# Graph layer with Performer mixer and two expert banks: basis parts, selection weights and the first weight piece in another order

## The reference, cut to what matters

```python
xn = layernorm(x)                                # x: 625 x 512
x  = x + gnn(xn) + mix(xn);  x = x + ffn(layernorm(x))

# gnn: two relational layers (relu between), 30 bases, 2 relations, 10000 edges
w = einsum('rb,bio->rio', att, basis)            # basis: 30 x 512 x 512
msg = where(edge_type == 0, sigmoid(x_j @ gate_w[0]) * x_j @ w[0],
                            sigmoid(x_j @ gate_w[1]) * x_j @ w[1])
out = segment_sum(msg, row) + x @ root + bias

# mix: Performer attention
k, q, v = split(layernorm_g1(xn) @ Wkqv + bkqv)
kp, qp = exp(k @ w.T - |k|^2/2) / 16, exp(q @ w.T - |q|^2/2) / 16
y = v + (qp @ (v.T @ kp).T / (qp @ sum(kp))) @ Wo + bo
y = y + gelu(layernorm_g2(y) @ W1 + b1) @ W2 + b2

# ffn: a shared expert and two banks of 8 experts, each node to one expert of each bank
```

## Time and profile before

| | |
|---|---|
| median of 3 runs | 550.5 us (549.6 to 551.97) |
| profiled execution | 551.3 us |
| its span (first to last instruction) | 549.5 us |
| granted TensorE clock, mean | 0.98 |
| TensorE busy | 501.2 us |
| VectorE, ScalarE, GpSimd busy | 250.6, 179.9, 175.0 us |
| moved by DMA | 104.66 MB |

### The profile page before, as it was taken

One profiled execution on the slowest core, in us unless ns is written; L12 is line 12 of the kernel. 1 busy time (PEld: TensorE's weight loads), 2 busy tenths in 40 slices (PEclk: granted clock), 3 DMA queues, 4 the chain that ended last, 5 costly groups with the idle time before them and its releaser, 6 DMA issues.

```text
span 549.5 us, 7975 instructions
## 1 busy us (share of the span) xinstructions
PE 501.2 (91%) x2842; PEld 372.5 (68%) x2842; DVE 250.6 (46%) x521; ACT 179.9 (33%) x366; POOL 175.0 (32%) x175
## 2 busy tenths in 40 slices
PE   2785899999999996989999999999988999999994
PEld 2342446777666644756677877777777888888883
DVE  4858871323534369332110123200275667766643
ACT  2795674222211118112220322401555123332210
POOL 2111000740503318460458150230253335533310
PEclk9997999999999998999999999999999799999998
DMA  5999997987999789657044004000020662222003
GB/s 123 420 397 413 424 421 260 366 305 232 370 411 403 259 325 372 236 202 271 1 108 160 0 1 107 14 2 0 1 78 1 255 276 78 78 76 78 1 1 94
DMA packets 27649, 104.66 MB, mean 190 GB/s; under 512 B 4152, under 2 KB 4197, under 8 KB 18908
## 3 DMA queue, kind: packets, MB, share of 16 engines
q1 hardware_dynamic: 27612, 104.16, 51.2%
HBM read 98.63 MB, written 5.51 MB: 190 GB/s over the span
## 4 chain that ended last, share of the span: by engine, by line
PE 82%; DVE 5%; DMA 4%; issue 3%; ACT 2%; SPq 2%; PEld 1%; DVEq 1%; PEldq 1%
PE ps L1235 19%; PE ps L1237 18%; PE ps L1236 18%; PE ps L1259 9%; PE ps L1596 9%; DMA ring<-in_L_gnn_basis_dram 3%; PE ps L1321 2%; PE ps L1441 2%; PE ps L1243 1%; PE ps L1499 1%; DMA out_dram<-final 1%; PEld ps L1321 1%; DVE oh_m L702 1%; ACT h_tmp L1023 1%; DVE oh_n L700 0%
## 5 line engine op out<-in xcount | busy, mean ns | idle before, releaser
L1259 PE MATMUL ps<-ring,sel_att 128*32 128x512 f32 x512 | 67.7, 616 | 11.2 <-DMA ring<-in_L_gnn_basis_dram 7.5
L602 POOL TENSOR_TENSOR ex_lo<-ex_raw,ex_hi 128x1024 fp32r<-128x1024 f32 x17 | 40.6, 2394 | 98.4 <-ACT ex_hi L1182 98.4
L852 DVE SCALAR_TENSOR_TENSOR u_lo<-ps,gates,u_hi 125x512 fp32r<-125x512 f32 x20 | 15.0, 751 | 94.1 <-ACT u_hi L1159 94.1
L1235 PE MATMUL ps<-piece_hi,ht_hi 128*125 128x512 f32 x140 | 56.1, 401 | 0.8 <-PE ps L1237 0.6
L1237 PE MATMUL ps<-piece_hi,ht_lo 128*125 128x512 f32 x140 | 55.2, 394 | 0.0
L1236 PE MATMUL ps<-piece_lo,ht_hi 128*125 128x512 f32 x140 | 55.1, 394 | 0.0
L913 DVE CAST hg_hi<-gated 128x314 fp32r<-128x314 f32 x32 | 35.6, 1113 | 32.0 <-PE ps L1237 31.4
L556 POOL CAST piece_hi<-piece_raw 128x512 fp32r<-128x512 f32 x28 | 20.4, 728 | 83.3 <-issue 60.2
L1235 PE MATMUL ps<-ht_hi,ex_hi 128*128 128x314 f32 x136 | 43.5, 320 | 0.0
L1237 PE MATMUL ps<-ht_hi,ex_lo 128*128 128x314 f32 x136 | 43.0, 316 | 0.0
L1236 PE MATMUL ps<-ht_lo,ex_hi 128*128 128x314 f32 x136 | 42.9, 315 | 0.0
(11 more groups left out here) (264 smaller groups left out, 1049.4 us busy)
## 6 DMA issues: line engine op xcount, KB each, us to landing
ring<-in_L_gnn_basis_dram SPq DMA_DIRECT2D x64, 1024.0 KB, 9.6
rel_dram<-stag SPq DMA_DIRECT2D x16, 256.0 KB, 7.9
w_raw<-rel_dram SPq DMA_DIRECT2D x8, 512.0 KB, 6.4
ex_raw<-in_L_ffn_W_sp_dram SPq DMA_DIRECT2D x16, 256.0 KB, 5.1
ex_raw<-in_L_ffn_W_fq_dram SPq DMA_DIRECT2D x16, 256.0 KB, 2.8
piece_raw<-in_L_mix_Wkqv_dram SPq DMA_DIRECT2D x3, 1024.0 KB, 8.7
route_all<-route_dram SPq DMA_DIRECT2D x1, 2512.0 KB, 12.0
piece_raw<-in_L_mix_W_dram SPq DMA_DIRECT2D x2, 1024.0 KB, 9.8
```

What stands on the lines that cost most here:

```text
L602: pool.tensor_tensor(lo, raw, hi.bitcast(F32), ALU.subtract).then_inc(ex_split, 1)
L1235: pe.matmul(target, a_hi, b_hi, start=first, stop=False, skip_group_check=skip)
L1259: last = pe.matmul(ps[32 * c:32 * c + 32, rel_bank(ch), :], sel_att[:, ch // CHUNKS, g].rearrange("p r q -> p (r q)"), ring[slot][:, c * D ...
```

## The change

Piece "k" is loaded behind part 11 rather than behind part 7, and the six bias rows behind part 32 rather than behind "k". GpSimd adds the two bias rows behind the split of "W1" rather than before that of "q". VectorE makes `sel_att` and the low half of the gate weights before it waits for the all-reduce, rather than after round 0. `k_lo` is made after VectorE's round 6 rather than its round 4. TensorE folds parts 0 and 1 before it waits for the ranges, and one part after round 0 rather than three.

```diff
@@ sync
             for i in range(4, 8):
                 load_part(i)
-            load_piece("k")
-            for n, a in enumerate((bias1, bias2, bkqv[2 * D:3 * D], bo, b2, bs2)):
-                sp.dma_start(bias_row[:, n, :], a.partition_broadcast(128)).then_inc(smalls_in, 16)
-
-            piece_after = {24: "q", 27: "v", 30: "Wo", 34: "W1", 40: "W2", 50: "root1", 62: "root2"}
+            piece_after = {11: "k", 24: "q", 27: "v", 30: "Wo", 34: "W1", 40: "W2", 50: "root1", 62: "root2"}
...
+                if i == 32:
+                    for n, a in enumerate((bias1, bias2, bkqv[2 * D:3 * D], bo, b2, bs2)):
+                        sp.dma_start(bias_row[:, n, :], a.partition_broadcast(128)).then_inc(smalls_in, 16)
@@ gpsimd
+            for name in ("q", "v", "Wo", "W1"):
+                split(name)
             pool.wait_ge(smalls_in, 16 * 6)
             own_step(pool.tensor_tensor(bias_row[:, 4, :], bias_row[:, 4, :], bias_row[:, 1, :], ALU.add))
-            for name in ("q", "v", "Wo", "W1"):
-                split(name)
@@ vector
+            dve.wait_ge(dve_own, sel_q_made)
+            dve.wait_ge(att_col_ready, 5)
+            a = sel_att[:].rearrange("p l g r q -> p (l g r) q")
+            dve.tensor_tensor(a, att_col[:]..., sel_q[:]..., ALU.mult).then_inc(sel_ready, 1)
+            dve.wait_ge(gate_w_hi, 1)
+            ...
+            dve.tensor_tensor(gate_w[:, :, 1, :], gate_ps, gate_w[:, :, 0, :].bitcast(F32), ALU.subtract).then_inc(gate_w_ready, 1)
             dve.wait_ge(bound_max, 1)
...
-                if j == 0:
-                    ...                       (the same steps)
-                if j == 4:
+                if j == 6:
                     _, p_hi, p_lo = piece("k")
@@ tensor
+            pe.wait_ge(sel_ready, 3)
+            relation_parts(2)
             pe.wait_ge(range_ready, 1)
             pe.wait_ge(consts_ready, 5)
...
-                if j == 0:
-                    pe.wait_ge(sel_ready, 3)
...
-                relation_parts(3 if j == 0 else 2)
+                relation_parts(1 if j == 0 else 2)
```

More of the change, by code:

```diff
@@ L672, in _ @@
             dve.tensor_tensor(router_fold[:], ident[0:4 * E, 0:2 * E], ident[0:4 * E, 2 * E:4 * E], ALU.add).then_inc(sel_ready, 1)
+            dve.wait_ge(dve_own, sel_q_made)
+            dve.wait_ge(att_col_ready, 5)
+            a = sel_att[:].rearrange("p l g r q -> p (l g r) q")
+            dve.tensor_tensor(a, att_col[:].rearrange("p l g r -> p (l g r)").unsqueeze(2).to_broadcast([128, 2 * NG * REL, QI]),
+                              sel_q[:].unsqueeze(1).to_broadcast([128, 2 * NG * REL, QI]), ALU.mult).then_inc(sel_ready, 1)
+            dve.wait_ge(gate_w_hi, 1)
+            gate_ps = ps[:, 5, 64:64 + 2 * KT * REL].rearrange("p (a r) -> p a r", r=REL)
+            gate_w = gate_hl[:].rearrange("p l t h r -> p (l t) h r")
+            dve.tensor_tensor(gate_w[:, :, 1, :], gate_ps, gate_w[:, :, 0, :].bitcast(F32), ALU.subtract).then_inc(gate_w_ready, 1)
             dve.wait_ge(bound_max, 1)
```

## The result

The changed kernel takes 558.72 us (median of 4 runs, 558.1 to 560.61) against 550.9 us (4 runs of before beside them, 549.6 to 551.97): ratio 1.0146, 95% interval [1.0122, 1.017], some 7.8 us more. The forecast was 552.5, its range up to 555.5: wrong. The profiled execution took 558.1 us, span 556.3, against 551.3 and 549.5.

A forecast was written before the change was run, and what follows sets the result against it. TensorE was taken as the bound (busy 501.2 of 549.5 us), with VectorE's one-hots and TensorE by turns before "k". 551.3 + 2.0 + 0 + 0 = 553.3 for the profiled execution, 552.5 for the median; range 549.6 to 555.5.

The forecast's parts named there:

- GpSimd's addition moves ... in front of a wait of 15.31 us: GpSimd's bias addition goes from 96 us to about 185, in front of a 15.31 us wait; no cost was counted.
- the sum: Counting rounds before "k": a 5.75 us late start shrinks to 3.2 at round 3, 1.35 at round 6; "k" +2.0.
- the release goes out when the parts' matmuls are issued: Start of counting: VectorE's first one-hot at 19.35 us, 5.75 later; 21.1 if the release waits for the matmuls' end.
- no wait for part 8: Before round 4: part 8 lands near 38.7 us instead of 47.0, so TensorE's 5.78 us wait goes.
- no late part behind the bias rows: Behind part 32: the late bias rows cost 0, part 35 having 3.5 us to spare; upper bound 2.3 us.
- rival C: Part 35 or 36 is waited for behind the bias rows: 2.3 us on top, 554.8 us; chance 0.04.
- the selection weights at 0: Selection weights ahead of the ranges fit into VectorE's 2.28 us all-reduce wait: cost 0, at most 0.6 us.
- `k_lo` behind round 6: VectorE's 2.49 us `k_lo` after round 6: lateness goes from 1.35 us at round 6 to 3.0 at round 7.
- that GpSimd alone would lose where its casts meet VectorE's one-hots: `k_hi`'s casts beside round 4's one-hots, 48.7 to 51 us: GpSimd loses; if VectorE lost instead, 2.28 us more.
- A: Late start kept: VectorE's chain stays late in rounds 5 and 6, `k_lo` adds 1.65: +4.85, 555.3 us; chance 0.12.
- B: DMA hole worth more: round 3 counted at 40, round 4 begun at 47.7: -1 to -2, 549 us; chance 0.10.
- D: Moves don't act: VectorE starts at 13.6 us, part 8's gain is lost behind parts 0 and 1: 550.5 us; 0.08.

The follow-up runs named there:

- Experiment 1: Kernel before with only the GpSimd order changed: bias rows added behind the split of W1 instead of before that of q; 553.2 us, ratio 1.0044.
- experiment 6: Kernel before with only the early selection weights and parts 0 and 1 ahead of the counting; 555.68 us, ratio 1.0085.
- experiment 4: Changed kernel with three parts after round 0 again and none ahead of the counting; 556.45 us, ratio 1.0102.
- experiment 11: Changed kernel with no part ahead, a small GpSimd tensor_tensor right behind the second all-reduce, and `k_lo` behind round 5; 551.42 us, ratio 1.0022.
- experiment 2: Changed kernel plus a 128 x 1 tensor_tensor on GpSimd directly behind the second all-reduce; 557.38 us, ratio 1.0124.
- experiment 3: Changed kernel with TensorE releasing the one-hot slots to VectorE before it folds parts 0 and 1; 561.09 us, ratio 1.0179.
- experiment 7: Kernel before with loads moved, bias addition behind W1, a small GpSimd tensor_tensor behind the all-reduce, and `k_lo` behind round 5; 551.99 us, ratio 1.0021.
- experiment 5: Changed kernel with 30 matmuls of a zero weight ahead of round 4, filling TensorE's hole; 558.78 us, ratio 1.0136.

## Why the prediction was wrong

**The step that failed first is "GpSimd's addition moves ... in front of a wait of 15.31 us" at a price of 0.** The addition itself was free there (it ran at 192.69 us in front of a wait of 14.12). But it had been the instruction that took the 10 us behind the all-reduce, and its row [10.05 <-DMA] looked like an ordinary wait. Experiment 1: 3.5 us in the stretch, 2.1 in the median.

**The second is the sum, "Here TensorE is the late one and most is won back".** TensorE is indeed mostly the late one there, but then its own delay stays, and little is won back. The sum let the delay shrink from 5.75 us at the first one-hot to 3.2 at round 3 and 1.35 at round 6; measured were 6.21, 5.15 and 4.30. In experiment 6 the rounds from 5 on keep 5.4 to 5.0 us behind those of before. The sum had "k" at 87.9, measured 90.80. The missing 2.9 by their place: first one-hot 19.81, not 19.35 (0.46); round 0 counted 7.0 us behind it, as before (20.57 against 13.60), where the sum gave 6.55 (0.46); in round 2 parts 3 and 4 ran to 34.87 and the two batches not back to back but 0.54 us apart (1.1); 8.1 us from round 3's last matmul to the first of round 4 instead of 7.7 (0.4), which is what VectorE lost beside GpSimd's casts; and gaps in rounds 4 to 9 (0.5 in all). These errors have one sign: the sum let an engine start when its input was ready and gave the gaps of one issue no length.

**Right:** the release goes out when the parts' matmuls are issued (19.81 lies before 21.2, their end); no wait for part 8; no late part behind the bias rows (part 35 landed at 155.98, used at 156.32 us: 0.34 to spare, not 3.5, so rival C was near: experiments 4 and 11 did wait for it, 0.25 and 0.80 us); the selection weights at 0.

**Half right:** `k_lo` behind round 6 was given +1.65. It cost 0.9 there (round 6 +4.30 over before, round 7 +5.18).

**Wrong, though small here:** that GpSimd alone would lose where its casts meet VectorE's one-hots. A row of GpSimd can't show what VectorE lost. Both lost: VectorE's ten pairs of round 4 took 0.4 us longer in the changed kernel, 1.1, 1.5 and 1.2 in experiments 2, 3 and 4, and no longer where the casts lay outside them. The bound of 2.28 us held.

**The rivals.** A said +4.85 at "k", measured +4.88, and its sign (round 6 counted later than 68: 69.67) came. Its reason was not the one: it wanted VectorE's chain late and 1.65 from `k_lo`; parts_ahead_only has the 5.0 without `k_lo` moved. So it met the number at "k" by luck, and its 555.3 lacks the GpSimd event. B is out by experiments 4 and 7: without any wait for part 8 the hole stays. D is out: one-hots from 19.81.

In us, of the profiled executions: forecast 553.3, +2.9 for the sum, +3.5 for the GpSimd event, +0.2 to part 63, -1.8 for the end's clock stretches, 558.1 measured. The median stands 0.6 above that execution, and the forecast for it had been put 0.8 below.

## What to carry to other kernels

Before an instruction is moved away from its place on GpSimd, look what the first arithmetic behind an all-reduce waits for: if it is 9 to 11 us that no input explains, whichever comes next inherits it, and a tiny instruction right behind the all-reduce, while the engine is idle, takes it up. Work put ahead of a chain that TensorE paces can cost its whole time, its wait for data included. An engine that waits for a later load may then run beside another engine and slow it. A wait that ends shortly before another input arrives is worth nothing: look at what is late next.

## What the runs showed of the hardware

Behind the second PARTITION_ALL_REDUCE GpSimd's next TENSOR_TENSOR is held up without any instruction in the profile: the idle time just before it is 9.24 to 11.33 us in the fourteen profiles. A CAST in between was not held up, and the gap came behind it (105.00 and 116.84 us in the changed kernel). The first all-reduce, before:

```profile
9.85 0.43 POOL L515 PARTITION_ALL_REDUCE bound_all<-bound  x1 [5.62 <-issue]
10.17 0.17 POOL L518 MEMSET ht_hi<- 128x12 f32 x1
19.13 0.28 POOL L522 TENSOR_SCALAR minus_mean<-mean_acc 125x5 f32<-125x5 f32 x1 [8.74 <-issue]
```

MEMSET ran at once. The 8.74 us are not such a gap as they stand, for the TENSOR_SCALAR needs the row sums of ScalarE, whose last one ended at 17.51 us:

```profile
17.32 0.19 ACT L991 ACTIVATION_READ_ACCUMULATOR xn<-xa 125x1 f32 x1
```

Only 1.62 us are left that no input explains (0.26 to 1.62 in the fourteen profiles). The start always lies 8.2 to 8.9 us behind the end of the all-reduce, which fits the same hold, but no run isolated it.

The Trainium skill (GPSIMD Engine Reference, "Instruction dispatch") says that the first call to a freshly loaded kernel of this engine pays about 6 us with no visible instruction. The gaps behind the second all-reduce are like that and longer; that loading code is their cause was not shown by any run.

VectorE's one-hots and GpSimd's casts slow each other when they overlap: an `oh_m` took 0.60 us instead of 0.24 and an `oh_n` 0.77 instead of 0.38 (experiment 3), four casts 3.23 us in experiment 4 instead of 2.28.

The granted clock fell to 0.50 in holes of TensorE of 4.95 to 6.05 us. Behind the wait for "q"'s split it fell in the changed kernel and in experiments 1 and 3 (waits of 2.01, 2.01 and 2.54 us), where the matmuls behind paid about 1.5 us more, and stayed at 1.00 in experiments 4 and 5 (2.01 and 1.64 us). Why it lasted 10.2 us in experiment 4 and 6.9 in experiment 11, with the same hole, stays open; so does where in the last 280 us the stretches at 0.50 come up.
